# Reordering the first attention pair, and moving the rounding of the first output tile to GpSimd in the last one

## The chip, the cores and the metric

One core of a Trainium2 chip. The metric is the time of one execution of the program on the device, in microseconds (us); smaller is better. Everything here is about single microseconds out of 570.

## What is computed

A block of a transformer on 2 batches of 512 tokens with width 512, in float32. It is an attention with low-rank (latent) queries, keys and values, and then a gated feed-forward layer; before and after each of the two stands a layer norm, and the sum goes on.

```python
q = (rmsnorm(hidden @ Wq_a) * w) @ Wq_b             # 32 heads, 128 plain + 64 rotated columns
ckv = hidden @ Wkv_a                                # 64 latent + 64 rotated columns
q_pe, k_pe = rope(q_pe), rope(k_pe)
scores = (qf @ kf.T) * scale, causal
o = softmax(scores) @ v                             # 32 heads
return o @ Wo
...
x = x + layernorm(attention(layernorm(x)))
x = x + layernorm(ffn(layernorm(x)))                # silu(gate) * up, low-rank additions
```

## The kernel before

Each engine has its own program, written out by hand, with semaphores between them. There is no scheduler: an instruction that waits holds back all that stands behind it in its engine's program.

Float32 products are made of three products of rounded parts. A value is split into a rounded "hi" (a copy on ScalarE, or on VectorE) and a "lo" (the value less its hi, a subtraction on VectorE or GpSimd). `three` on TensorE then multiplies hi by hi, hi by lo and lo by hi.

The attention runs over 16 pairs of heads (`body(p)`). A pair has 16 steps k: eight for batch 0 and eight for batch 1, four query blocks for each of two heads. One unit of work is numbered U = 16p + k. Its stages, and the engines:

- `scores` (TensorE) makes the scores of unit U, two steps ahead of the step that turns them. Unit 4g (i = 0) needs the rotated query g (`pe_added`); unit 4g + 1 needs the query's lo part as well (`qt_split`). It also waits until the mask of unit U - 2 has emptied its bank (`s_masked`).
- `mask_and_max` (VectorE, L804) adds the causal mask and takes the row maximum. One input is in PSUM, the other in SBUF.
- `exponent` (ScalarE, L500), then `turn_p` (TensorE, L1249) transposes, `move_p` (ScalarE, L508) brings the result to SBUF, and `output` (TensorE, L1261) multiplies the values once for every eight units. `invert`, `turn_r`, `move_r` and `scale_o` divide by the row sums.

The queries of a pair come from `query` (TensorE, five products of 512 columns, L1179 to L1222). It needs the pair's weights in both parts: `weights_hi` (ScalarE, four roundings, L476 to L479), `weights_lo` (VectorE, L779 and L780), `rope_lo` (GpSimd, L395 and L398). A query is then rotated: `rotate_swapped` (VectorE, two half-tile products, L789 and L790), `rotate_own` (VectorE, L796), `add_rotated` (GpSimd, L382). Then it is split: `query_hi` (ScalarE, L490) and `query_lo` (GpSimd, L389). In the first pair, queries 0 and 1 (batch 0) are made in the stage before the attention; queries 2 and 3 (batch 1) are rotated and split inside `body(0)`, and queries 4 and 5 are the next pair's.

In the last pair (`last=True`) there is nothing left to prepare, so that work on the output projection is put in between: `split_weights` makes the parts of 16 projection weights (weights 0 to 5 wholly on VectorE, with a cast L826 and a subtraction L830; the rest with the rounding on ScalarE, L523), `split_output` splits a tile of the attention's output (L532 on ScalarE, L836 on VectorE, 1024 columns each), and `project` multiplies them on TensorE. The weights come back from a scratch in DRAM, through three buffers, in eight loads (L341): the load of weights 14 and 15 starts when weight 9 is split. `project(0, 0)` multiplies weights 0 to 7 with the first half of tile 0.

Of the kernel before, what the change touches and what calls it, by code (L numbers as in the profile page):

```python
# [20 lines left out]
F32 = mybir.dt.float32  # L21
# [65 lines left out]
def build(nc, x_d, wa_d, lnw_d, cst_d, kcs_d, sq_d, sv_d, w13_d, bs_d, a13_d, a2_d, w2_d, b2_d, out_d):  # L87
# [141 lines left out]
    def sems(phase, words):  # L229
        return Semaphores((n, nc.alloc_semaphore(f"{phase}_{n}")) for n in words.split())  # L230
# [12 lines left out]
    c = sems("projection", """xn2_made wv_in0 wv_in1 wv_in2 wv_copied wv_hi_made wv_split o_hi_made o_split o_used x1_first x1_in w13_in bs_in a13_in  # L243
# [9 lines left out]
    with block:  # L253
# [114 lines left out]
        def _(pool):  # L368
# [33 lines left out]
            def body(p, last=False):  # L402
                for b in (1,) if last else (1, 0):
                    for h in range(2):
                        gi = 4 * p + (2 if b else 4) + h
                        pool.wait_ge(a.qt_split, gi)
                        add_rotated(gi, h)
                        if b and h == 0 and not last:
                            pool.wait_ge(a.pe_added, gi + 1)
                            rope_lo(p + 1)  # L410
                        query_lo(gi, b, h, gi + 1)
# [22 lines left out]

# [27 lines left out]
        def _(act):  # L463
# [94 lines left out]
            def body(p, first=False, last=False):  # L558
                for k in range(PU):
                    if last and k == 6:  # L560
                        split_output(0, 0)
# [19 lines left out]
                    if k in ((2, 4) if first else (1, 4)):  # L581
                        h = k // 4
                        query_hi(4 * p + 2 + h, 1, h, None if first else PU * (p - 1) + UNITS + QB * (h + 1))
# [77 lines left out]
            exponent(1, 1, True)  # L661
            move_p(0, 0)
            exponent(2, 2, True)
            query_hi(1, 0, 1)
# [108 lines left out]
        def _(dve):  # L773
# [9 lines left out]
            def rotate_swapped(gi, h, first=False):  # L783

                dve.wait_ge(a.q_made, gi + 1)
                if not first:
                    dve.wait_ge(a.pe_added, gi - 1)
                G = bank[6 + h]
                nc.vector.tensor_tensor(qswp[64:96, h, :], G[96:128, :], sin1[96:128, :], ALU.mult)  # L789
                nc.vector.tensor_tensor(qswp[96:128, h, :], G[64:96, :], sin1[64:96, :], ALU.mult)  # L790
# [42 lines left out]
            def split_output(t, hh):  # L833

                dve.wait_ge(c.o_hi_made, 2 * t + hh + 1)
                nc.vector.tensor_tensor(o_s[:, hh, 1, :, :], ot[:, t, 8 * hh:8 * hh + 8, :],  # L836
                                        o_s[:, hh, 0, :, :].bitcast(F32), ALU.subtract).then_inc(c.o_split, 1)
# [8 lines left out]
            def body(p, first=False, last=False):  # L846
                for k in range(PU):
# [7 lines left out]
                    if last and k == 7:  # L855
                        split_output(0, 0)
# [3 lines left out]
                    if k < UNITS or not last:  # L860
                        if first and k in (1, 2):
                            rotate_swapped(gi + k - 1, k - 1)
                            if k == 1:
                                rotate_own(gi, 0)
                        elif first and k == 3:
                            weights_lo(p + 1)
                            rotate_own(gi + 1, 1)
# [34 lines left out]
            for t in range(TB + 4):  # L902
                if 2 <= t - 2 < TB:
                    turned_lo(t - 2)
                if 0 <= t - 3 < TB:
# [28 lines left out]
                if t == 7:  # L934
                    weights_lo(0)
                if 0 <= t - 4 < TB:
# [13 lines left out]
                if t in (TB, TB + 3):  # L950
                    h = (t - TB) // 3
                    rotate_swapped(h, h, first=True)
                    rotate_own(h, h, first=True)
# [222 lines left out]
        def _(pe):  # L1176
# [230 lines left out]
            body(PAIRS - 1, last=True)  # L1407
            output(2 * PAIRS - 1, 1, range(QB))
# [14 lines left out]
            project(0, 0, (6, 7))  # L1423
# [165 lines left out]
```

## Time and profile before

| | us |
|---|---|
| median of 3 runs (lowest, highest) | 570.12 (569.55, 570.97) |
| the profiled execution | 569.77 |
| its span, first to last instruction | 568.20 |
| TensorE busy | 555.2 (98%) |
| VectorE busy | 444.4 (78%) |
| ScalarE busy | 396.7 (70%) |
| GpSimd busy | 212.3 (37%) |

The first pair runs from about 41 us to 60 us, the last from about 382 us to 406 us, and the projection follows. A busy share is an average over all of these; what a change is worth can only be read in the stretch where it acts. TensorE's clock was granted at 0.997 of full over the span.

### The profile page before, as it was taken

To read this page: it belongs to the slowest core of one execution; us is meant where nothing else is said; L and a number is where in the kernel's file an instruction comes from. 1 tells how busy PE (TensorE), PEld (TensorE's weight loads), DVE (VectorE), ACT (ScalarE), POOL (GpSimd) and SP (SyncE) were. 2 spreads that over 40 slices of the span, in tenths; PEclk is the share of its full clock that TensorE was granted. 3 is DMA by queue.
4 is the path that set the end of the run, shared out by engine and by line. 5 is a ranking of instruction groups with operands and counts; after the bars stand their busy time and mean duration, and the time that the engine had idled before them with its cause. 6 is when DMAs were issued, how large, how long until landed. Compare 5 with 4: busy or idle time off the path is not lost. (4 is left out here: it accounts for less than half of the span.)

```text
span 568.2 us, 10892 instructions
## 1 busy us (share of the span) xinstructions
PE 555.2 (98%) x3280; PEld 423.4 (75%) x3280; DVE 444.4 (78%) x1198; ACT 396.7 (70%) x1173; POOL 212.3 (37%) x221
## 2 busy tenths in 40 slices
PE   8999999999999999999999999999999999999996
PEld 7777778777787787778877877876778888755565
DVE  5978777787777777877787788788878989885476
ACT  4767778787888787878888887888745554274353
POOL 3225454344443543444445435533011112135730
PEclk9999999999999999999999999999999999999998
DMA  8911232213312222111102101004591000001003
GB/s 325 407 64 66 81 101 82 79 53 99 112 53 80 78 106 80 53 50 59 53 21 71 52 20 45 22 21 149 190 347 58 2 14 1 1 1 55 1 35 115
DMA packets 22025, 46.93 MB, mean 83 GB/s; under 512 B 2896, under 2 KB 5712, under 8 KB 21712
## 3 DMA queue, kind: packets, MB, share of 16 engines
q1 hardware_dynamic: 21968, 46.23, 23.7%
q8 instruction: 28, 0.46, 0.3%
q14 instruction: 29, 0.24, 0.1%
HBM read 39.80 MB, written 6.42 MB: 81 GB/s over the span
## 5 line engine op out<-in xcount | busy, mean ns | idle before, releaser
L804 DVE CUSTOM_DVE_ANT_0 ss<-bank,cst 128x128 f32<-128x128 f32 (+3 forms) x256 | 125.1, 489 | 71.8 <-PE bank L1181 40.3
L508 ACT ACTIVATE pt<-bank 128x128 f32<-128x128 f32 (+3 forms) x256 | 110.2, 430 | 62.7 <-PE bank L1249 62.3
L500 ACT ACTIVATE pr<-ss,small 128x128 f32<-128x128 f32 (+3 forms) x256 | 143.0, 558 | 7.1 <-DVE small L804 5.6
L382 POOL TENSOR_TENSOR qrot<-qrot,qswp 64x512 f32<-64x512 f32 x64 | 82.2, 1284 | 115.9 <-DVE qrot L796 113.5
L1249 PE MATMUL bank<-ident,pr 128*128 128x128 f32 x640 | 113.6, 275 | 0.6 <-ACT pr L500 0.5
L1249 PEld LDWEIGHTS bank<-ident,pr 128*128 128x128 f32 x640 | 78.5, 141 | 22.2 <-issue 5.3
L389 POOL TENSOR_TENSOR qt_lo<-qrot,qt_hi 128x384 fp32r<-128x384 f32 x64 | 64.6, 1009 | 71.1 <-ACT qt_hi L490 70.0
L1179 PE MATMUL bank<-kt_hi,qt_hi 128*128 128x256 f32 (+2 forms) x192 | 80.9, 421 | 1.4 <-POOL qt_lo L389 0.7
L1261 PE MATMUL bank<-pt,kvn 128*64 128x256 f32 (+3 forms) x512 | 75.2, 434 | 0.7 <-ACT pt L508 0.7
L1261 PEld LDWEIGHTS bank<-pt,kvn 128*64 128x64 f32 x512 | 38.6, 137 | 40.6 <-issue 28.2
L1181 PE MATMUL bank<-kt_hi,qt_lo 128*128 128x256 f32 (+2 forms) x192 | 65.1, 339 | 0.0
L1180 PE MATMUL bank<-kt_lo,qt_hi 128*128 128x256 f32 (+2 forms) x192 | 64.7, 337 | 0.0
L1179 PE MATMUL bank<-wv,o_s 128*128 128x512 f32 x128 | 51.5, 402 | 0.0
L1181 PE MATMUL bank<-wv,o_s 128*128 128x512 f32 x128 | 50.5, 395 | 0.0
L1180 PE MATMUL bank<-wv,o_s 128*128 128x512 f32 x128 | 50.4, 394 | 0.0
L500 ACT ACTIVATION_READ_ACCUMULATOR pr<-ss,small 128x1 f32 x256 | 49.7, 194 | 0.0
L789 DVE TENSOR_TENSOR qswp<-bank,cst 32x512 f32<-32x512 f32 x64 | 44.5, 696 | 2.0
L790 DVE TENSOR_TENSOR qswp<-bank,cst 32x512 f32<-32x512 f32 x64 | 44.2, 691 | 0.9
L796 DVE TENSOR_TENSOR qrot<-bank,cst 128x512 f32<-128x512 f32 x64 | 43.9, 686 | 0.1
L438 POOL TENSOR_TENSOR half<-xn 128x256 f32<-128x256 f32 x7 | 8.1, 1157 | 89.9 <-ACT xn L550 79.9
L1179 PEld LDWEIGHTS bank<-kt_hi,qt_hi 128*128 128x128 f32 x192 | 36.4, 190 | 4.8 <-issue 1.6
L1181 PEld LDWEIGHTS bank<-kt_hi,qt_lo 128*128 128x128 f32 x192 | 36.1, 188 | 2.8
(189 smaller groups left out, 1113.8 us busy)
## 6 DMA issues: line engine op xcount, KB each, us to landing
rsb<-rinv_scratch SPq DMA_DIRECT2D x64, 128.0 KB, 2.9
sv<-sv SPq DMA_DIRECT2D x9, 576.0 KB, 4.5
sqa<-sq SPq DMA_DIRECT2D x16, 320.0 KB, 3.2
wv_raw<-wvo_scratch SPq DMA_DIRECT2D x8, 512.0 KB, 4.2
sve<-sv SPq DMA_DIRECT2D x7, 576.0 KB, 9.6
wvo_scratch<-vs SPq DMA_DIRECT2D x10, 256.0 KB, 2.2
xa<-x SPq DMA_DIRECT2D x8, 256.0 KB, 6.0
sqr<-sq SPq DMA_DIRECT2D x16, 128.0 KB, 2.2
```

What stands on the lines that cost most here:

```text
L382: nc.gpsimd.tensor_tensor(qrot[RKV:P, h, :], qrot[RKV:P, h, :], qswp[RKV:P, h, :], ALU.add)\
L389: nc.gpsimd.tensor_tensor(qt_lo[:, b, h, P:SEQ], qrot[:, h, P:SEQ], qt_hi[:, b, h, P:SEQ].bitcast(F32), ALU.subtract)\
L500: nc.scalar.activation(pr[:, k % 4, 0:n], ss[:, RING[k], 0:n], ACT.Exp, bias=negmax[:, k % 8:k % 8 + 1], scale=-1.0, accum_out=rsum[:, k:k ...
L508: nc.scalar.activation(pt[:, b, h, 0:i + 1, i * P:(i + 1) * P], bank[2 + k % 2][:, 0:(i + 1) * P].rearrange("p (j q) -> p j q", q=P), ACT. ...
L789: nc.vector.tensor_tensor(qswp[64:96, h, :], G[96:128, :], sin1[96:128, :], ALU.mult)
L790: nc.vector.tensor_tensor(qswp[96:128, h, :], G[64:96, :], sin1[64:96, :], ALU.mult)
L804: nc.vector.tensor_tensor_reduce(out=ss[:, RING[k], 0:n], in0=bank[k % 2][:, 0:n], in1=mask[:, SEQ - n:SEQ], scale=-SCALE, scalar=3.4e38, ...
L1179: nc.tensor.matmul(out, w_hi, x_hi, start=start, stop=False)
L1180: nc.tensor.matmul(out, w_hi, x_lo, start=False, stop=False)
L1181: return nc.tensor.matmul(out, w_lo, x_hi, start=False, stop=stop)
L1249: last = nc.tensor.transpose(bank[2 + k % 2][:, j * P:(j + 1) * P], pr[:, k % 4, j * P:(j + 1) * P], ident[:, :])
L1261: last = nc.tensor.matmul(bank[4][RKV * h:RKV * (h + 1), j * P:SEQ], kvn[:, QB * b + j, 0:RKV], pt[:, b, h, j, j * P:SEQ], start=(j == 0), ...
```

## The change

In the first pair and just ahead of it:

- VectorE rotates query 1 earlier: its two half-tile products go, one each, ahead of the latent scaling in the two last steps but one of the first stage, and `rotate_own` ahead of the last latent split. Before, all three stood behind mask 1.
- VectorE takes queries 2 and 3 in pieces between the masks: query 2's own product goes from step 1 to step 3, query 3's two halves from step 2 to steps 4 and 5, its own product from step 3 to step 5, and `weights_lo(1)` from step 3 to step 4.
- ScalarE does `query_hi` of query 1 ahead of `move_p(0)` and the third exponent; `query_hi` of queries 2 and 3 goes from steps 2 and 4 to steps 5 and 7, behind the exponents of units 7 and 9.
- GpSimd does `rope_lo(1)` ahead of `add_rotated` of query 2, not behind it.

In the last pair:

- The split of the first output tile's first half leaves ScalarE (step 6) and VectorE (step 7). GpSimd does it behind its last query: two copies of 512 columns and a subtraction of 1024 columns.
- TensorE's `project(0, 0)` for weight 6 goes from behind the last values product to ahead of it.

```diff
                     for h in range(2):
                         gi = 4 * p + (2 if b else 4) + h
                         pool.wait_ge(a.qt_split, gi)
+                        if b and h == p == 0:
+                            rope_lo(1)
                         add_rotated(gi, h)
-                        if b and h == 0 and not last:
+                        if b and h == 0 and p and not last:
                             pool.wait_ge(a.pe_added, gi + 1)
                             rope_lo(p + 1)
                         query_lo(gi, b, h, gi + 1)
...
+            pool.wait_ge(a.q_made, 4 * PAIRS)
+            pool.wait_ge(a.o_scaled, PAIRS + 2)
+            for n in (slice(0, 4), slice(4, 8)):
+                nc.gpsimd.tensor_copy(o_s[:, 0, 0, n, :], ot[:, 0, n, :]).then_inc(c.first_hi_made, 1)
+            pool.wait_ge(c.first_hi_made, 2)
+            nc.gpsimd.tensor_tensor(o_s[:, 0, 1, :, :], ot[:, 0, 0:8, :], o_s[:, 0, 0, :, :].bitcast(F32), ALU.subtract)\
+              .then_inc(c.o_split, 1)
...
                 for k in range(PU):
-                    if last and k == 6:
-                        split_output(0, 0)
...
-                    if k in ((2, 4) if first else (1, 4)):
-                        h = k // 4
+                    if k in ((5, 7) if first else (1, 4)):
+                        h = k // 7 if first else k // 4
                         query_hi(4 * p + 2 + h, 1, h, None if first else PU * (p - 1) + UNITS + QB * (h + 1))
...
             exponent(1, 1, True)
+            query_hi(1, 0, 1)
             move_p(0, 0)
             exponent(2, 2, True)
-            query_hi(1, 0, 1)
...
-                dve.wait_ge(c.o_hi_made, 2 * t + hh + 1)
+                dve.wait_ge(c.o_hi_made, 2 * t + hh)
...
-                    if last and k == 7:
-                        split_output(0, 0)
...
-                        if first and k in (1, 2):
-                            rotate_swapped(gi + k - 1, k - 1)
+                        if first and 0 < k < 6:
                             if k == 1:
+                                rotate_swapped(gi, 0)
+                            if k == 3:
                                 rotate_own(gi, 0)
-                        elif first and k == 3:
-                            weights_lo(p + 1)
-                            rotate_own(gi + 1, 1)
+                            if k == 4:
+                                weights_lo(p + 1)
+                            if k in (4, 5):
+                                rotate_swapped(gi + 1, 1, parts=(k - 4,))
+                            if k == 5:
+                                rotate_own(gi + 1, 1)
...
+                if t in (TB + 1, TB + 2):
+                    rotate_swapped(1, 1, True, (t - TB - 1,))
...
+                if t == TB + 3:
+                    rotate_own(1, 1, first=True)
...
-                if t in (TB, TB + 3):
-                    h = (t - TB) // 3
-                    rotate_swapped(h, h, first=True)
-                    rotate_own(h, h, first=True)
+                if t == TB:
+                    rotate_swapped(0, 0, first=True)
+                    rotate_own(0, 0, first=True)
...
             body(PAIRS - 1, last=True)
+            project(0, 0, (6,))
             output(2 * PAIRS - 1, 1, range(QB))
...
-            project(0, 0, (6, 7))
+            project(0, 0, (7,))
```

## Rows read from the trace of the kernel before

**Rows 1.** Busy time by stretch: start:end, length, then PE, PEld, DVE, ACT, POOL

```profile
60.00:383.00 323.00, 323.00 (x2101) 252.96 (x2098) 250.61 (x714) 260.55 (x852) 143.69 (x143) 1.00 0.20 64
```

**Rows 2.** Waits of TensorE, 41 to 60 us: total, times, longest

```profile
PE bank L1179 <- POOL qt_lo L389: 0.7, 1, 0.7
PE bank L1179 <- DVE small L804: 0.6, 1, 0.6
```

**Rows 3.** Timeline of TensorE, first pair and second: start, duration, instruction, idle before

```profile
46.23 0.49 PE L1249 MATMUL bank<-ident,pr 128*128 128x128 f32 x3
...
50.60 0.39 PE L1179 MATMUL bank<-ql_hi,w_hi 128*128 128x512 f32 x1
...
51.75 0.38 PE L1249 MATMUL bank<-ident,pr 128*128 128x128 f32 x2
...
52.55 0.36 PE L1179 MATMUL bank<-kt_hi,qt_hi 128*128 128x256 f32 x1
...
56.59 0.46 PE L1235 MATMUL bank<-kt,qrot 128*128 128x128 f32 x2
...
76.45 0.37 PE L1179 MATMUL bank<-kt_hi,qt_hi 128*128 128x256 f32 x1
...
80.13 0.39 PE L1235 MATMUL bank<-kt,qrot 128*128 128x128 f32 x2
```

**Rows 4.** Timeline of VectorE, end of the first stage and first pair

```profile
36.12 0.17 DVE L912 RECIPROCAL st<-st 128x2 f32<-128x2 f32 x1 [0.86 <-ACT st L624]
...
47.58 0.28 DVE L804 CUSTOM_DVE_ANT_0 ss<-bank,cst 128x128 f32<-128x128 f32 x1
```

**Rows 5.** Timeline of ScalarE, first pair

```profile
48.30 0.29 ACT L476 ACTIVATE w_hi<-sqr 128x128 fp32r<-128x128 f32 x1
...
52.70 0.52 ACT L490 ACTIVATE qt_hi<-qrot 128x384 fp32r<-128x384 f32 x1 [0.50 <-POOL qrot L382]
...
53.39 0.71 ACT L500 ACTIVATE pr<-ss,small 128x512 f32<-128x512 f32 x1
```

**Rows 6.** Timeline of GpSimd, first pair

```profile
53.36 1.02 POOL L389 TENSOR_TENSOR qt_lo<-qrot,qt_hi 128x384 fp32r<-128x384 f32 x1 [0.70 <-ACT qt_hi L490]
```

**Rows 7.** Waits of TensorE, 383 to 415 us

```profile
PE bank L1261 <- ACT pt L508: 0.7, 1, 0.7
PE bank L1270 <- ACT pr L500: 0.5, 1, 0.5
```

**Rows 8.** Timeline of VectorE, last pair and after it

```profile
392.01 1.23 DVE L836 TENSOR_TENSOR o_s<-ot,o_s 128x1024 fp32r<-128x1024 f32 x1 [0.74 <-ACT o_s L532]
...
393.63 0.42 DVE L826 CAST wv<-wv_raw 128x512 fp32r<-128x512 f32 x1
...
401.88 0.69 DVE L830 TENSOR_TENSOR wv<-wv_raw,wv 128x512 fp32r<-128x512 f32 x1
...
413.42 1.23 DVE L836 TENSOR_TENSOR o_s<-ot,o_s 128x1024 fp32r<-128x1024 f32 x1 [0.18 <-ACT o_s L532]
```

**Rows 9.** GpSimd's instructions by line and shape: total busy us, mean ns of one

```profile
L389 POOL TENSOR_TENSOR qt_lo<-qrot,qt_hi 128x384 fp32r<-128x384 f32 x64 | 64.6, 1009 | 71.1 <-ACT qt_hi L490 70.0
...
L395 POOL TENSOR_TENSOR w_lo<-sqr,w_hi 128x128 fp32r<-128x128 f32 x16 | 7.4, 460 | 8.9 <-ACT w L477 8.9
...
L419 POOL COPY qn<-qn 128x64 f32<-128x64 f32 x8 | 1.9, 238 | 0.0
```

**Rows 10.** Timeline of GpSimd, then of VectorE, 420 to 426 us

```profile
422.50 1.14 POOL L438 TENSOR_TENSOR half<-xn 128x256 f32<-128x256 f32 x1 [31.30 <-ACT xn L550]
...
422.97 1.23 DVE L1000 CUSTOM_DVE_ANT_0 dot<-xn,a 128x512 f32<-128x512 f32 x1
```

**Rows 11.** Timeline of TensorE, end of the last pair and projection

```profile
403.13 0.48 PE L1179 MATMUL bank<-wv,o_s 128*128 128x512 f32 x1
...
414.70 0.50 PE L1179 MATMUL bank<-wv,o_s 128*128 128x512 f32 x1
```

**Rows 12.** Timeline of ScalarE, start of the projection

```profile
411.28 1.16 ACT L523 ACTIVATE wv<-wv_raw 128x512 fp32r<-128x512 f32 x2 [1.11 <-DMA wv_raw<-wvo_scratch]
```

More of the change, by code:

```diff
@@ L242, in build @@
         wvo_made wvo_moved wvo_out""")
-    c = sems("projection", """xn2_made wv_in0 wv_in1 wv_in2 wv_copied wv_hi_made wv_split o_hi_made o_split o_used x1_first x1_in w13_in bs_in a13_in
+    c = sems("projection", """xn2_made wv_in0 wv_in1 wv_in2 wv_copied wv_hi_made wv_split first_hi_made o_hi_made o_split o_used x1_first x1_in w13_in bs_in a13_in
         dve_step std1_made z_made std2_made half_made fold_made dots_raw dots_made lt_zero y_turned xt2_moved lp_hi_made lp_split""")
@@ L781, in weights_lo, with rotate_swapped @@
                   .then_inc(a.wq_split, 1)
-            def rotate_swapped(gi, h, first=False):
+            def rotate_swapped(gi, h, first=False, parts=(0, 1)):
                 dve.wait_ge(a.q_made, gi + 1)
@@ L787, in rotate_swapped @@
                     dve.wait_ge(a.pe_added, gi - 1)
-                G = bank[6 + h]
-                nc.vector.tensor_tensor(qswp[64:96, h, :], G[96:128, :], sin1[96:128, :], ALU.mult)
-                nc.vector.tensor_tensor(qswp[96:128, h, :], G[64:96, :], sin1[64:96, :], ALU.mult)
+                for j in parts:
+                    to, of = 64 + 32 * j, 96 - 32 * j
+                    nc.vector.tensor_tensor(qswp[to:to + 32, h, :], bank[6 + h][of:of + 32, :], sin1[of:of + 32, :], ALU.mult)
             def rotate_own(gi, h, first=False):
```

## The prediction, made before the changed kernel was run

> **What bounds the kernel now.** I read the busy times by stretch first. From 60 to 383 us TensorE is busy for 323.00 of 323.00 us [rows 1]: there it is the bound, it has no gap, and whatever delay it has at 60 us it still has at 383. So I then read TensorE's waits in the two stretches that the change touches. In the first pair they are 0.7 us for the lo part of query 1 and 0.6 us for a mask [rows 2]; at the end of the last pair 0.5 us before the transposed row sums and 0.7 us for the last `move_p` [rows 7]. That is all there is to win: some 2.5 us, plus a little refill of the pipeline. Then I walked through both stretches by the timelines of the engines, since every one of these waits ends a chain over VectorE, ScalarE and GpSimd, and the change reorders those chains.
>
> **Query 1, earlier.** Its rotation costs VectorE three products. They go into gaps: one half into 0.86 us in which VectorE waits for ScalarE [rows 4], the others into two like it of 0.72 and 1.06 us in the next two steps; a half takes 0.70 us, so they just fit, and cost nothing. If a gap were missed, what is late is a latent split, by some 0.1 us. The own product is then ready by 40.8 us, GpSimd adds by 42.1, and the lo part is done at about 44.4 instead of 47.4. The score product of unit 5 can start 0.25 us behind the transposes at 46.23 [rows 3] instead of at 47.46: TensorE is 1.0 us ahead.
>
> **Up to query 4.** Mask 4 no longer has query 2's own product (0.61 us) in front of it and starts at 47.0 instead of 47.58 [rows 4]. Exponent 4 and `weights_hi(1)` behind it on ScalarE are 0.6 us earlier too: 47.7 instead of 48.30 [rows 5], done 0.8 us later at 48.5. VectorE is free for `weights_lo(1)` (two of 0.3 us) at 48.7 and done at 49.3. On GpSimd `rope_lo(1)`, two of 0.46 us [rows 9], starts 0.15 us behind the rope roundings at 48.2 and is done at about 49.35, since it now goes ahead of the addition. So query 4 starts at 49.4 instead of 50.60 [rows 3]. TensorE waits there for 0.7 us, and is 1.2 us ahead. `add_rotated` of query 2, now behind `rope_lo`, is done at 50.7, just when the score product of unit 8 wants it (50.8): no loss.
>
> **Unit 9, the place where it turns.** That product needs the lo part of query 2. Before, its rounding stood at step 2 of ScalarE's program, long ahead. Now it stands at step 5, behind `move_p(5)` and the exponent of unit 7, and `move_p(5)` needs transposes that TensorE makes behind query 4. The chain from query 4's start: 1.15 us to the transposes (50.60 to 51.75) [rows 3] and 0.38 until they are done, 51.0; on ScalarE the move, the exponent (0.71) and the rounding (0.52), 0.69 of which are the step from 52.70 to 53.39 [rows 5], so 1.5 us in all, 52.5; 0.15 us and 1.02 us on GpSimd [rows 6], 53.7. Before, the product started at 52.55 [rows 3]. Without this chain it could start at 51.3; with it TensorE stands for 2.4 us and comes out 1.15 us behind the kernel before. From 52.55 to 56.59 the kernel before takes 4.04 us for pieces that take 3.68 us in the second pair (76.45 to 80.13) [rows 3]; these 0.36 us are small waits that a later TensorE doesn't meet. So the first pair costs 0.8 us, with 1.2 us as the upper end (nothing given back) and 0.4 us as the lower (each of the five hand-overs of the chain 0.08 us shorter). The rounding of query 3, behind exponent 9, has slack: its lo part is ready at 58.6, and unit 13 comes at 61.
>
> **The first output tile on GpSimd.** ScalarE loses its 1.05 us, so that exponent 8 starts almost 1 us earlier and the 0.5 us wait at the row sums [rows 7] is gone: TensorE is 0.8 us ahead from 392.1 us. VectorE loses 1.23 us at 392.01 [rows 8], but mask 10 behind it needs scores that are ready at 392.3, so it gains 0.9. GpSimd starts at 391.3, behind its last `query_lo`. The subtraction: 384 columns take 1.009 us and 128 take 0.460 [rows 9], 2.15 ns a column, so 1024 take 2.4 us. A copy of 512 columns isn't in the trace. Lower bound 0.6 us (0.238 for 64 columns [rows 9], the other 448 at 0.8 ns); upper bound 1.3 us (the subtraction's rate). I take 0.75, as the one copy that is there takes three quarters of a short two-input instruction but has one input to read. The copies end at 392.8, the subtraction at 395.3 to 395.7. Weight 0's product wants it at 396.6: in time, up to copies of 1.2 us. *A page's price:* the Trainium skill, GPSIMD Engine Reference, § 3.1, gives 769 ns for 512 elements of a tight one-input loop; by that the sum is the same 571.6.
>
> **What GpSimd's subtraction does to VectorE.** In the projection GpSimd's addition starts at 422.50 and lasts until 423.64; VectorE's instruction with both inputs in SBUF starts at 422.97 and takes 1.23 us instead of its 0.69, that is it ends 0.55 us behind GpSimd's end [rows 10]. So VectorE stood until GpSimd was through. Masks and rotations have one input in PSUM and keep their durations beside GpSimd all through the attention. In the last pair VectorE starts splitting weights behind mask 10: cast and subtraction, both from SBUF. With the cast at 392.8 and GpSimd's subtraction starting at about 392.9 either way round, weight 0's parts are done at about 396.2 and mask 11 starts there, instead of at 394.69: VectorE is 1.5 us late. And it has no slack: from 393.15 to 404.4 it goes from mask to split to mask with gaps of 0.2 us in all. Weight 5's lo part was done at 402.57, 0.56 us ahead of its product at 403.13 [rows 8, 11]. So 1.5 less 0.2 less 0.56: TensorE is 0.7 us late at weight 5's product, and its 0.8 us lead is lost on the way. Bounds: 0.8 us early (VectorE isn't held up), 1.7 us late (copies of 1.3 us, cast and subtraction both held up). 
>
> **Weight 6's product ahead of the last values.** 0.7 us of TensorE's work goes into its 0.7 us wait for `move_p(15)` [rows 7]. But the gain isn't kept: the first product of tile 1, at 414.70 [rows 11], starts right behind the split of that tile, which ends at 413.42 + 1.23 = 414.65 [rows 8]. This split hangs on ScalarE's last two weights, which wait 1.11 us for their load [rows 12], which waits for weight 9's split, which is behind `move_p(15)`. That chain starts at the transposes of unit 15 and doesn't become shorter. TensorE comes to it 0.7 us early and waits: 0 us gained, 0.1 at most.
>
> **Sum.** +0.8 + 0.7 + 0 = +1.5 us. The profiled execution took 569.77 us, 568.20 of them its span; it becomes 571.3. The median of the runs is 0.35 us above it, so I forecast 571.6 us, and by the ends of the terms (0.4 less 0.8, and 1.2 and 1.7) 569.7 to 573.0, its own likely range 570.8 to 572.4. A measurement of this kernel tells a change of about 0.3%, 1.7 us, from none.
>
> **Rivals.**
>
> 1. *GpSimd doesn't hold up VectorE.* For: most of GpSimd's work in the attention costs VectorE nothing. Against: the instruction at 422.97 [rows 10]. The last pair then keeps its 0.8 us lead, the first costs 0.8: 570.1 us. Chance 0.2.
> 2. *It does what it says.* The lo part of query 2 comes in time and so all four waits go: 1.0 + 0.6 + 0.8 + 0.7 us, 567.0 us. It needs the rounding of query 2 to be done 2.4 us earlier than its place in ScalarE's program allows. Chance 0.1.
> 3. *Slower: VectorE becomes the bound of the last pair.* With copies of 1.2 us or more, GpSimd holds the port to 396.6; VectorE is 2.5 us late, and TensorE waits at the scores of unit 13 and again at weights 4 and 5: +1.7 us there, +1.0 in the first pair, 572.8 us. It decides from the point where cast and subtraction both wait, copies of about 1.0 us. Chance 0.2.
>
> The forecast has 0.45; 0.05 is left for what I don't see. Faster by over 0.3% (below 568.4) holds rival 2: 0.1. Slower by over 0.3% (above 571.8) holds rival 3 and four tenths of the forecast: 0.38. The rest, 0.52, is no change. For 8 in 10 the range runs from 569.0, which takes in rival 1, to 573.0.
>
> **What would show it.** First pair: TensorE's wait for `qt_lo` moves from unit 5 to unit 9 and grows to 2.4 us; query 4 starts 1.2 us earlier; the product of unit 12 starts 0.8 us later than 56.59. Last pair: GpSimd's subtraction takes 2.4 us or more; one cast or subtraction of VectorE near 393 us takes over 2 us; mask 11 starts at 396.2; no wait for ScalarE's row sums; TensorE waits for VectorE's weight 5, and for the split of tile 1. The prediction is wrong in sign if unit 9 doesn't wait, or if VectorE's weight splits keep 0.42 and 0.69 us.

## The result, and the profile after

The changed kernel takes 572.71 us (median of 5 runs, 571.00 to 573.21); the kernel before took 569.97 us in the runs beside it. The ratio is 1.0041, 95% interval 1.003 to 1.0051: slower by 0.4%. The forecast was 571.6 us, in a range of 569.0 to 573.0. One execution each of three kernels further below (the second form of both mended halves, weight 6 alone, the subtraction in halves) took 689 to 1931 us, and the ratios leave these three out.

| | before | after |
|---|---|---|
| span of the profiled execution, us | 568.2 | 570.7 |
| TensorE busy, us | 555.2 | 557.7 |
| VectorE, ScalarE, GpSimd busy, us | 444.4, 396.7, 212.3 | 444.9, 395.4, 215.8 |

TensorE is busy for 2.5 us longer although it executes the same 3280 matmuls. 0.8 us of that lies in the first 10 us, ahead of every edit (8.47 against 7.67 us busy), but 1.3 us lies between the first latent transposes and unit 12 (21.27 against 19.97). That is the first sign that it isn't only a matter of waits: a wait makes an engine idle, not busy. All line numbers have moved in the changed kernel: the helper `three`, L1179 to L1181 before, is L1191 to L1193, `turn_p` (L1249) is L1261, and the unit products L1235 are L1247.

**First pair.** TensorE's waits from 41 to 62 us, in total, times, longest (before: [rows 2]):

```profile
PE bank L1191 <- POOL qt_lo L389: 2.2, 1, 2.2
PE bank L1191 <- DVE w L787: 0.5, 1, 0.5
```

The wait for a lo part is no longer at unit 5, but at unit 9, three times as long. TensorE's timeline shows what it does around it (start, duration, instruction, idle before and its releaser; before: [rows 3]):

```profile
46.73 0.49 PE L1261 MATMUL bank<-ident,pr 128*128 128x128 f32 x3
46.98 0.36 PE L1191 MATMUL bank<-kt_hi,qt_hi 128*128 128x256 f32 x1
...
49.97 0.47 PE L1191 MATMUL bank<-ql_hi,w_hi 128*128 128x512 f32 x1 [0.54 <-DVE w L787]
...
54.30 0.39 PE L1191 MATMUL bank<-kt_hi,qt_hi 128*128 128x256 f32 x1 [2.17 <-POOL qt_lo L389]
...
55.54 0.63 PE L1193 MATMUL bank<-ql_hi,w_lo 128*128 128x512 f32 x1
55.97 0.63 PE L1233 MATMUL bank<-ql_hi,w 128*128 128x512 f32 x1
...
59.59 0.39 PE L1247 MATMUL bank<-kt,qrot 128*128 128x128 f32 x2
```

Unit 5 now follows its transposes by 0.25 us. Query 4 is 0.63 us earlier than before, unit 9 is 1.75 us later. And then come two lines that a list of waits doesn't have: products of 512 columns that take 0.63 us and follow each other by 0.43 us, where the same ones at 50.50 us took 0.39 and followed by 0.23. From unit 9 to unit 12 TensorE needs 59.59 − 54.30 = 5.29 us for pieces that take 3.68 us in the second pair [rows 3]. The windows of this stretch say why (start:end, length, then busy time of PE, PEld, DVE, ACT, POOL, the granted clock of TensorE, and DMA):

```profile
50.00:52.00 2.00, 2.00 (x12) 1.63 (x12) 1.94 (x5) 1.16 (x6) 1.24 (x1) 1.00 0.45 101
52.00:54.00 2.00, 0.13 (x2) 0.00 (x0) 0.81 (x3) 1.87 (x6) 0.75 (x1) 1.00 0.33 128
54.00:56.00 2.00, 1.71 (x7) 1.42 (x8) 1.02 (x4) 0.00 (x0) 1.52 (x2) 0.70 0.00 0
56.00:58.00 2.00, 2.00 (x9) 1.70 (x7) 0.91 (x2) 0.09 (x1) 0.00 (x0) 0.50 0.00 0
58.00:60.00 2.00, 2.00 (x14) 1.62 (x15) 1.34 (x4) 2.00 (x7) 0.44 (x1) 0.94 0.00 0
```

and of the kernel before, in the two that matter:

```profile
54.00:56.00 2.00, 2.00 (x14) 1.53 (x12) 1.72 (x4) 2.00 (x9) 0.38 (x1) 1.00 0.00 0
56.00:58.00 2.00, 1.98 (x12) 1.00 (x12) 1.97 (x6) 1.62 (x7) 0.81 (x1) 1.00 0.01 2
```

The granted clock is 0.70 and 0.50 behind the standstill. 0.50 is half of full speed, 1.2 GHz in place of 2.4; 0.70 is the mean of a window that began at full speed. Before it fell, TensorE had stood still from 52.13 to 54.30. The Trainium skill (TensorE: Matmul & The Clock Gate, Part 1) names the same two levels, and an idle stretch as what leads to the lower one; the trace agrees as to both, 0.50 behind a wait of 2.17 us.

The chain that makes unit 9 wait, on ScalarE and then on GpSimd (before: [rows 5, 6]):

```profile
51.62 0.38 ACT L517 ACTIVATE pt<-bank 128x256 f32<-128x256 f32 x1 [0.84 <-PE bank L1261]
51.90 0.71 ACT L509 ACTIVATE pr<-ss,small 128x512 f32<-128x512 f32 x1
...
52.60 0.51 ACT L499 ACTIVATE qt_hi<-qrot 128x384 fp32r<-128x384 f32 x1
```

```profile
53.25 0.99 POOL L389 TENSOR_TENSOR qt_lo<-qrot,qt_hi 128x384 fp32r<-128x384 f32 x1 [2.01 <-ACT qt_hi L499]
```

ScalarE stands before `move_p(5)` for transposes that TensorE makes behind query 4, and the rounding of query 2 is queued behind it.

**Last pair.** GpSimd's new copies and its subtraction, then VectorE (before: [rows 8, 9]):

```profile
394.01 1.17 POOL L440 CAST o_s<-ot 128x512 fp32r<-128x512 f32 x2
395.26 2.38 POOL L442 TENSOR_TENSOR o_s<-ot,o_s 128x1024 fp32r<-128x1024 f32 x1
```

```profile
395.65 2.27 DVE L833 CAST wv<-wv_raw 128x512 fp32r<-128x512 f32 x1
...
398.57 0.68 DVE L811 CUSTOM_DVE_ANT_0 ss<-bank,cst 128x512 f32<-128x512 f32 x1
399.18 0.08 DVE L811 DVE_READ_ACCUMULATOR2_ANT small<- 128x1 f32 x1
399.18 0.42 DVE L833 CAST wv<-wv_raw 128x512 fp32r<-128x512 f32 x1
```

One and the same cast takes 0.42 us at 399.18 and 2.27 us at 395.65, where it ends 0.28 us behind GpSimd's subtraction (395.26 + 2.38 = 397.64, 395.65 + 2.27 = 397.92). Mask 11 stands behind it.

Weight 5's product and tile 1's first product on TensorE, and the load behind tile 1 on ScalarE (before: [rows 11, 12]):

```profile
406.37 0.48 PE L1191 MATMUL bank<-wv,o_s 128*128 128x512 f32 x1 [0.47 <-DVE wv L837]
...
417.38 0.39 PE L1191 MATMUL bank<-wv,o_s 128*128 128x512 f32 x1
```

```profile
413.84 1.16 ACT L532 ACTIVATE wv<-wv_raw 128x512 fp32r<-128x512 f32 x2 [0.33 <-DMA wv_raw<-wvo_scratch]
```

**Where the time went.** The same instruction of TensorE stands in both traces, so the difference of its two starts is the delay up to there, and the steps between are the cost of each stretch. The first row, the start-up, is by how much the whole trace is later ahead of any edit:

| up to | before | after | delay | step | forecast |
|---|---|---|---|---|---|
| first latent transposes | 35.04 | 35.26 | 0.22 | start-up | – |
| transposes ahead of unit 5 | 46.23 | 46.73 | 0.50 | +0.28 | 0 |
| query 4 | 50.60 | 49.97 | −0.63 | −1.13 | −1.2 |
| unit 9 | 52.55 | 54.30 | 1.75 | +2.38 | +2.35 |
| unit 12 | 56.59 | 59.59 | 3.00 | +1.25 | −0.36 |
| turn of the last pair | 386.41 | 389.28 | 2.87 | −0.13 | 0 |
| weight 5's product | 403.13 | 406.37 | 3.24 | +0.37 | +0.7 |
| tile 1's first product | 414.70 | 417.38 | 2.68 | −0.56 | 0 |

### The profile page after: what moved, and what is told of

It reads as the page before. It is cut to its first block, busy times and chain, and to the rows that moved or that the text cites. A ratio compares the mean times of both kernels' runs of the same rounds, so it can differ in the third digit from the quotient of the medians.

```text
span 570.7 us, 10896 instructions
## 1 busy us (share of the span) xinstructions
PE 557.7 (98%) x3280; PEld 425.4 (75%) x3280; DVE 444.9 (78%) x1197; ACT 395.4 (69%) x1172; POOL 215.8 (38%) x224
## 3 DMA queue, kind: packets, MB, share of 16 engines
q1 hardware_dynamic: 21968, 46.23, 23.7%
## 4 chain that ended last, share of the span: by engine, by line
PE 81%; DVE 12%; ACT 3%; issue 3%; POOL 0%; DVEq 0%; POOLq 0%; ACTq 0%
PE bank L1191 14%; PE bank L1193 13%; PE bank L1192 13%; PE bank L1261 12%; PE bank L1273 12%; DVE dot L1012 3%; PE bank L1288 3%; PE bank L1234 3%; PE bank L1233 3%; PE bank L1247 2%; PE bank L1213 1%; DVE st L986 1%; DVE o_s L843 1%; PE bank L1471 1%; ACT o_s L541 1%
## 5 line engine op out<-in xcount | busy, mean ns | idle before, releaser
L1261 PE MATMUL bank<-ident,pr 128*128 128x128 f32 x640 | 113.9, 276 | 0.6 <-ACT pr L509 0.5
L1261 PEld LDWEIGHTS bank<-ident,pr 128*128 128x128 f32 x640 | 79.0, 141 | 22.0 <-issue 5.5
L1191 PE MATMUL bank<-kt_hi,qt_hi 128*128 128x256 f32 (+2 forms) x192 | 81.2, 423 | 2.3 <-POOL qt_lo L389 2.2
L1193 PE MATMUL bank<-kt_hi,qt_lo 128*128 128x256 f32 (+2 forms) x192 | 65.0, 339 | 0.0
L1191 PE MATMUL bank<-wv,o_s 128*128 128x512 f32 x128 | 51.6, 403 | 0.5 <-DVE wv L837 0.5
L1193 PE MATMUL bank<-wv,o_s 128*128 128x512 f32 x128 | 50.5, 395 | 0.0
L1191 PEld LDWEIGHTS bank<-kt_hi,qt_hi 128*128 128x128 f32 x192 | 36.6, 190 | 5.7 <-POOL qt_lo L389 2.4
L1193 PEld LDWEIGHTS bank<-kt_hi,qt_lo 128*128 128x128 f32 x192 | 36.2, 188 | 2.8
L1192 PEld LDWEIGHTS bank<-kt_lo,qt_hi 128*128 128x128 f32 x192 | 37.0, 193 | 0.0
```

The source lines that it names most:

```text
L1191: nc.tensor.matmul(out, w_hi, x_hi, start=start, stop=False)
L1192: nc.tensor.matmul(out, w_hi, x_lo, start=False, stop=False)
L1193: return nc.tensor.matmul(out, w_lo, x_hi, start=False, stop=stop)
L1261: last = nc.tensor.transpose(bank[2 + k % 2][:, j * P:(j + 1) * P], pr[:, k % 4, j * P:(j + 1) * P], ident[:, :])
```

## The experiments

Two theories stood at the start. A: the whole loss is made in the first pair, by the wait at unit 9 and by the lower clock behind it, and the last pair costs next to nothing. B: the last pair, through VectorE's held-up cast, costs its share of some 0.7 us. Each kernel was timed in rounds with the kernel before on the same chip (its median was 570.0 or 570.1 us in each of the three series).

### The first pair alone, the last pair alone

The change has two halves that touch different stretches; each kernel here is the kernel before with one of them (the hunks on `rotate_swapped`, `rotate_own`, `query_hi`, `rope_lo` and `weights_lo` in the one, the rest in the other).

> The kernel before with the edits of the first pair alone. Theory A (what the trace of the changed kernel says): the pieces moved ahead cost 0.25 us, the chain to the score product of unit 9 costs 0.8 us, and TensorE's clock at half speed behind the long wait costs 1.6 us, so +2.6 us: about 572.6 us, with the product of unit 12 about 2.7 us later than in the kernel before. Theory B (the slow stretch of the clock is not tied to the wait, an accident of that execution): only the chain, +1.0 us, 571.0 us.

> The kernel before with the edits of the last pair alone. Theory A: weight 6's product does fill the wait, and the load of the last weights comes 0.6 us sooner behind its trigger than I reckoned, so that the pair ends 0.2 us early: 569.8 us, TensorE's first product of tile 1 at 414.5. The forecast's reckoning: +0.7 us, 570.7 us, that product at 415.4, with TensorE waiting for the split of tile 1.

Measured: 572.88 us for the first pair alone, ratio 1.005 (1.0033 to 1.0066), and 570.36 us for the last pair alone, ratio 1.0006 (0.9997 to 1.0016). The first pair alone makes the whole loss, near the 572.6 us of theory A. Its windows show the lower clock again, and its timeline shows it from the first product behind the wait (0.29 us to the next product where the changed kernel has 0.22):

```profile
54.00:56.00 2.00, 1.67 (x6) 1.47 (x7) 0.68 (x4) 0.00 (x0) 1.55 (x2) 0.61 0.00 0
56.00:58.00 2.00, 2.00 (x9) 1.60 (x8) 1.26 (x2) 0.00 (x0) 0.00 (x0) 0.53 0.00 0
```

```profile
54.33 0.49 PE L1188 MATMUL bank<-kt_hi,qt_hi 128*128 128x256 f32 x1 [2.17 <-POOL qt_lo L389]
54.62 0.42 PE L1189 MATMUL bank<-kt_lo,qt_hi 128*128 128x256 f32 x1
```

In the last pair alone the cast is held up in the same way, and TensorE comes to tile 1's first product 0.53 us behind the kernel before, having entered the pair 0.30 us behind it: the pair costs 0.23 us net. I had expected this pair either to end 0.2 us early or to cost 0.7 us. It does neither: the product is at 415.23, behind a wait of 0.28 us for its split, and the interval of the time holds no change.

```profile
393.08 2.25 DVE L831 CAST wv<-wv_raw 128x512 fp32r<-128x512 f32 x1
...
395.98 0.68 DVE L809 CUSTOM_DVE_ANT_0 ss<-bank,cst 128x512 f32<-128x512 f32 x1
```

### Is it the standstill that costs, or what comes of it?

The wait and the clock come together. To part them, TensorE gets work without a use in the wait; the wait itself isn't touched. This is the changed kernel with

```diff
                     n = k + 2
+                    if first and n == 9:
+                        for _ in range(20):
+                            nc.tensor.transpose(bank[XB][:, 0:P], ident[:, :], ident[:, :])
                     if n < PU:
```

> The changed kernel, and on TensorE 20 transposes of the identity (0.11 us each, 2.1 us in all) ahead of the score product of unit 9, so that TensorE works while it waits. Nothing else changes, and the product still starts when its lo part is there. Theory A (the clock falls because TensorE stands still): the granted clock stays at 1.0 from 54 to 59 us, the pieces behind unit 9 take 3.7 us and not 5.3, and the time is 1.6 us below the changed kernel's: 571.1 us. Theory B (something else slows these pieces): the clock falls again and the time is the changed kernel's, 572.7 us.

Measured: 571.64 us, ratio 1.0021 (1.0004 to 1.0039), 1.1 us less than the changed kernel though TensorE does more. The two intervals overlap (1.003 to 1.0051 for the changed kernel), so it is the trace that decides. The timeline of TensorE:

```profile
51.95 2.35 PE L1322 MATMUL bank<-ident 128*128 128x128 f32 x20
54.30 0.39 PE L1191 MATMUL bank<-kt_hi,qt_hi 128*128 128x256 f32 x1
...
55.22 0.39 PE L1193 MATMUL bank<-ql_hi,w_lo 128*128 128x512 f32 x1
...
58.00 0.28 PE L1247 MATMUL bank<-kt,qrot 128*128 128x128 f32 x1
```

Unit 9 starts at 54.30, as in the changed kernel, but unit 12 is at 58.00 and no longer at 59.59; the pieces take 3.70 us, the 3.68 us of the second pair, and a product of 512 columns takes 0.39 us. The granted clock is 1.00 in all windows from 52 to 60 us. The standstill itself costs 2.2 us, and the clock that it leads to costs 1.6 us on top. That is shown for these traces: nothing but the idleness was taken away. I had expected 571.1 us. TensorE is still 1.56 us ahead of the changed kernel at the turn of the last pair (387.72 against 389.28), but only 1.21 us at tile 1's first product (416.17 against 417.38), where it waits 0.21 us for its split, behind a load of the last weights that took 0.5 us longer (below).

The lower clock may not come in every execution. Of the five timed ones of the changed kernel, four took 572.35 to 573.21 us at a mean granted clock of 0.994 to 0.997, and the fifth took 571.00 us at 0.999. That is what a run without the fall would give, but no trace of it was kept.

### Rounding one step earlier

The wait is a matter of one place in ScalarE's program. The changed kernel with

```diff
-                    if k in ((5, 7) if first else (1, 4)):
+                    if k in ((4, 7) if first else (1, 4)):
```

> The changed kernel with the rounding of query 2 on ScalarE at step 4 in place of 5, that is ahead of the move of unit 5 and the exponent of unit 7. Theory A (the place of the rounding makes the wait): the addition is done at 51.25, the rounding at 51.8, the lo part at 53.0, so that TensorE waits 0.9 us at unit 9 and not 2.2; 1.3 us less, and if the clock stays up another 1.6: 570.0 us, or 571.4 if it falls even so. Theory B (GpSimd's order, the rope part ahead of the addition, makes the wait): the lo part comes at 54 as before, 572.7 us.

Measured: 569.94 us, ratio 1.0001 (0.9991 to 1.001). One digit takes the whole loss back, as theory A had it. The rounding now stands ahead of `move_p(5)` and its wait for TensorE; unit 9 still waits, but its wait of 0.85 us doesn't bring the clock down (1.00 in all windows from 52 to 58 us):

```profile
52.94 0.38 PE L1191 MATMUL bank<-kt_hi,qt_hi 128*128 128x256 f32 x1 [0.85 <-POOL qt_lo L389]
...
56.67 0.39 PE L1247 MATMUL bank<-kt,qrot 128*128 128x128 f32 x2
```

Unit 12 is at 56.67 against 56.59 before.

### Query 1 alone

What is the early rotation of query 1 worth? The kernel before with the hunks for query 1 only (its two halves and its own product in the first stage, its rounding ahead of `move_p(0)`).

> The kernel before with one edit alone: the rotation of query 1 is done early, in pieces, and its rounding stands ahead of move_p(0); the order inside the first pair stays. Theory B (the lo part of query 1 isn't the last thing late): the 0.7 us wait at unit 5 is gone, but query 4 still waits for its weights, whose chain over mask 4, exponent 4 and the roundings is unchanged, so it starts within 0.3 us of 50.60 on the trace; the three pieces ahead of the first latent scaling cost the 0.25 us that the changed kernel shows there, or nothing if TensorE waits for the weights in any case. Time 570.0 to 570.3. Rival: unit 5's gain is kept, query 4 starts at 49.6 to 49.9 and the time is 569.0 to 569.4.

Measured: 570.25 us, ratio 1.0003 (0.9994 to 1.0012). TensorE's waits and timeline:

```profile
PE bank L1182 <- DVE small L804: 1.4, 2, 1.0
```

```profile
46.87 0.36 PE L1182 MATMUL bank<-kt_hi,qt_hi 128*128 128x256 f32 x1
...
50.99 0.40 PE L1182 MATMUL bank<-ql_hi,w_hi 128*128 128x512 f32 x1
```

Unit 5 follows its transposes by 0.25 us in place of 1.23, so 1.0 us is gained there, and by query 4 it is all given back, 50.99 against 50.60 (0.29 us later, net of a start-up of 0.10), in waits for VectorE's masks: the wait for `qt_lo` has turned into waits for `small`. At the turn of the last pair this kernel is 0.2 us later than the start-up accounts for, which is the price of the three early pieces. So an early query 1 gains nothing by itself. That it pays together with what makes query 4 earlier is likely, but not shown: no run has the rest without it.

### The first pair with the chain in another order

If the two chains (weights to query 4, query 2 to unit 9) set the pair, both must be shortened. Both kernels are the kernel before with the change's first-pair hunks, and these steps in place of its own (`weights_hi(1)`, then `query_hi`, then VectorE's pieces inside the pair, and query 1's in the first stage):

```diff
-                    if k == (2 if first else 1) and not last:
+                    if k == 1 and not last:
...
-                    if k in ((2, 4) if first else (1, 4)):
+                    if k in ((3, 7) if first else (1, 4)):
...
+                            if k == 2:
+                                rotate_own(gi, 0)
+                            if k == 3:
+                                weights_lo(p + 1)
...
+                if t == TB + 1:
+                    rotate_swapped(1, 1, True, (0,))
...
+                if t == TB + 3:
+                    rotate_swapped(1, 1, True, (1,))
+                    rotate_own(1, 1, first=True)
```

This is the second of them; the first has query 2's own product at step 3 and its rounding at step 4.

> The edits of the first pair alone, with other steps: query 2's and 3's rounding at steps 4 and 7, weights_hi(1) on ScalarE at step 1 and weights_lo(1) on VectorE at step 3, and query 1's second half behind the latent scaling rather than ahead of it. Theory (first pair is a chain over weights, query 4, and the rounding of query 2; the clock falls only if TensorE stands for long at unit 9): query 4 starts at 48.9 to 49.5, unit 9 at 51.6 to 52.3 with a wait under 1.2 us, granted clock 1.00, so 0.3 to 0.9 us ahead of the kernel before: 569.1 to 569.7. Rival (each us gained in front is given back by the rounding): unit 9 at 52.9 as with step 4 alone, 569.9 to 570.1.

> As the run before, with query 2's own product at step 2 and its rounding at step 3. Theory: unit 9 at 50.9 to 51.5, 1.0 to 1.5 us ahead of the kernel before, 568.6 to 569.1. Rival: the own product in front of mask 3 makes the scores of unit 5 or the turn of unit 4 late, weights and query 4 follow, and the gain is under 0.5 us: 569.5 to 570.0.

Measured: 569.34 us, ratio 0.9986 (0.9978 to 0.9995), and 569.33 us, ratio 0.9986 (0.9977 to 0.9994). TensorE in the second:

```profile
49.41 0.40 PE L1189 MATMUL bank<-ql_hi,w_hi 128*128 128x512 f32 x1
...
51.43 0.39 PE L1189 MATMUL bank<-kt_hi,qt_hi 128*128 128x256 f32 x1
...
52.68 0.47 PE L1189 MATMUL bank<-ql_hi,w_hi 128*128 128x512 f32 x1 [0.63 <-DVE qrot L798]
```

Query 4 is 1.2 us and unit 9 1.1 us earlier than before, and unit 9 doesn't wait. What is late next is query 5: its product overwrites the bank from which VectorE still reads query 3, whose pieces now stand at steps 4 and 5. Both kernels are 1.0 us ahead of the start-up's offset at the turn of the last pair, 0.7 us in the time. My expectations for the places in the first were missed (query 4 at 48.9 to 49.5, unit 9 at 51.6 to 52.3): they are at 49.96 and 52.82, but its whole trace is 1.1 us late from the start-up on. Its time was met. For the second it is the other way round: unit 9 at 51.43 was met, and the time of 569.33 us lies between the 568.6 to 569.1 of the theory and the 569.5 to 570.0 of its rival. One step earlier for query 2 didn't show in the time, since query 5 is the next to wait.

### GpSimd's copies in its own gap

The last pair's edits alone, but with GpSimd's two copies ahead of its last `query_lo`, in the 1.5 us for which it stands there:

```diff
+                        if last and h:
+                            pool.wait_ge(a.q_made, 4 * PAIRS)
+                            pool.wait_ge(a.o_scaled, PAIRS + 2)
+                            pool.wait_ge(a.pe_added, gi + 1)
+                            for n in (slice(0, 4), slice(4, 8)):
+                                nc.gpsimd.tensor_copy(o_s[:, 0, 0, n, :], ot[:, 0, n, :]).then_inc(c.first_hi_made, 1)
+                            pool.wait_ge(c.first_hi_made, 2)
                         query_lo(gi, b, h, gi + 1)
```

> The kernel before with the edits of the last pair alone, but with GpSimd's two copies ahead of its last query_lo, in the 1.5 us in which it stands for the rounding, so that its subtraction starts some 1.2 us earlier (about 391.5). Theory (the time of the last pair's edit hangs on how long GpSimd's subtraction holds VectorE's first cast): the cast takes 0.9 to 1.4 us instead of 2.25, mask 11 is at 394.6 to 395.0, TensorE doesn't wait for weight 5, and its entry offset of 0 to 0.3 us is what is left: 569.3 to 569.9. Rival (the load of the last weights sets the end of this stretch whatever the masks do): the cast is shorter but tile 1's first product stays at 414.7 to 415.2, 570.0 to 570.4.

Measured: 569.25 us, ratio 0.9992 (0.9978 to 1.0005). GpSimd, VectorE and TensorE:

```profile
389.10 1.17 POOL L416 CAST o_s<-ot 128x512 fp32r<-128x512 f32 x2 [0.16 <-POOL qrot L382]
...
391.58 2.39 POOL L443 TENSOR_TENSOR o_s<-ot,o_s 128x1024 fp32r<-128x1024 f32 x1
```

```profile
393.06 1.20 DVE L834 CAST wv<-wv_raw 128x512 fp32r<-128x512 f32 x1
...
394.90 0.68 DVE L812 CUSTOM_DVE_ANT_0 ss<-bank,cst 128x512 f32<-128x512 f32 x1
```

```profile
414.11 0.50 PE L1185 MATMUL bank<-wv,o_s 128*128 128x512 f32 x1 [0.24 <-DVE o_s L844]
```

The subtraction starts 1.10 us earlier (391.58 against 392.68) and the cast, at the same place to 0.02 us, becomes 1.05 us shorter. In each of the three traces (and in the two of both mended halves) the cast ends 0.28 or 0.29 us behind GpSimd's subtraction. So the hold-up is a matter of where the subtraction ends, not of how much GpSimd does. Tile 1's first product is 0.59 us ahead of the kernel before and was 0.27 us behind on entry, so the last pair gains 0.9 us. Places and theory agree; the time is just under the 569.3 to 569.9 us that I had expected, and its interval alone doesn't part this kernel from the one before.

### Weight 6's product alone

The kernel before with `project(0, 0, (6,))` ahead of the last `output`, `(7,)` behind it, and nothing else.

> The kernel before with one edit alone: weight 6's product ahead of the last values. Theory of the prediction (the split of tile 1 behind the load of the last weights sets the end): the wait for move_p(15) is gone, weight 8's product is 0.6 to 0.7 us earlier, tile 1's first product waits for its split and stays within 0.15 us of 414.70 plus the entry offset; time 570.0 to 570.2. Rival (the load comes earlier too, as the runs of the last pair alone hint): tile 1's product at 414.1 to 414.4, 569.4 to 569.7.

Measured: 569.87 us, ratio 0.9996 (0.9986 to 1.0006). TensorE, and ScalarE's last weights:

```profile
408.59 0.50 PE L1179 MATMUL bank<-wv,o_s 128*128 128x512 f32 x1
...
414.83 0.50 PE L1179 MATMUL bank<-wv,o_s 128*128 128x512 f32 x1 [0.35 <-DVE o_s L836]
```

```profile
411.42 1.16 ACT L523 ACTIVATE wv<-wv_raw 128x512 fp32r<-128x512 f32 x2 [1.10 <-DMA wv_raw<-wvo_scratch]
```

Weight 8's product is 0.4 us earlier (409.00 before; 0.5 us net of the delay on entry, where I had expected 0.6 to 0.7), tile 1's first product is where it was (414.83 against 414.70, with 0.12 us of entry delay), behind a new wait for the split. Taken alone the edit is worth nothing, as forecast.

### The subtraction in halves

The last pair's edits as in the change, with the subtraction in two instructions of 512 columns.

> The edits of the last pair as in the change, but GpSimd's subtraction of 1024 columns made in two instructions of 512. Theory (VectorE's cast is held for what is left of the one GpSimd instruction that runs, not for a queue of them): GpSimd's first half takes 1.2 us, and the cast that meets it takes 0.9 to 1.4 us instead of 2.25; GpSimd's second half and VectorE's subtraction then take turns, so mask 11 is at 395.0 to 396.3 instead of 396.1 and the time 569.6 to 570.3. Rival (GpSimd keeps VectorE out over both halves): the cast takes 2.2 us or more again and the time is 570.2 to 570.6.

Measured: 570.23 us, ratio 0.9996 (0.9986 to 1.0005), against 570.36 us (1.0006, 0.9997 to 1.0016) in one piece. The intervals overlap, the time is within the span that both theories gave, and there is no trace from which the places could be read, so whether the cast is held over both halves stays open.

### Both mended halves together

> Both edits in their mended form in one kernel: the first pair as in the run with query 2's own product at step 2, the last pair as in the run with GpSimd's copies ahead of its last lo part. Theory (TensorE has no gap from 60 to 383 us, so what the two ends gain adds up): minus 0.7 and minus 0.8 us, 568.5 to 568.8. Rival (an earlier TensorE at the last pair meets an end that is set by the load of the last weights, so the second gain is smaller): 569.0 to 569.4.

> The same with the other form of the first pair (own product at step 3, rounding at step 4). Both theories as for the run before; 568.5 to 568.8 if the gains add up, 569.0 to 569.4 if the load of the last weights takes one back.

Measured: 568.07 us, ratio 0.996 (0.9944 to 0.9975), and 568.38 us, ratio 0.9964 (0.995 to 0.9978). Both beat the kernel before and the changed one. The gains add up: in the first, TensorE enters the last pair 1.25 us ahead of the kernel before (385.16 against 386.41; 1.04 us net of the start-up) and comes to tile 1 2.53 us ahead:

```profile
412.17 0.41 PE L1195 MATMUL bank<-wv,o_s 128*128 128x512 f32 x1
```

```profile
408.67 1.16 ACT L535 ACTIVATE wv<-wv_raw 128x512 fp32r<-128x512 f32 x2 [0.34 <-DMA wv_raw<-wvo_scratch]
```

The times are 0.4 and 0.1 us below the lower end of what I expected. The load of the last weights waited for is shorter here (below), which helps in the trace; the interval of the time, −1.4 to −3.2 us, holds the sum of the two parts (−1.5 us) as well.

## Why the prediction was right, and where its sum was not

The sign and the range held, and so did the place: the wait for `qt_lo` moves to unit 9. Most terms of the first pair came out to a tenth of a microsecond. But two terms were wrong in opposite directions, and the sum of 1.5 us was too small against 2.7 us in the medians (2.3 us by the ratio). That the time stayed inside the range is in part luck: the first pair cost more than twice its own upper end of 1.2 us, and the range had room for it only because it held 1.7 us for a last pair that cost next to nothing.

- **Query 1, early: cost put at 0, 0.1 at most.** It costs 0.2 to 0.3 us: the transposes ahead of unit 5 are 0.28 us later than the start-up accounts for, and in the run with query 1 alone 0.2 us stay. The pieces fitted into VectorE's idle time, but the latent scaling behind them came a little late, and TensorE shows a new 0.27 us wait for `qn` at 37.85 us.
- **Up to query 4: −1.2 us, measured −1.13.** Right, with `weights_lo` done at 49.73 and `rope_lo` as the last to come at 49.87 (I had 49.35, and the trace was 0.50 us late there), a wait of 0.54 us. The profile puts the wait down to `weights_lo`, but by their ends it is `rope_lo`.
- **Unit 9: wait of 2.4 us, 1.15 us behind.** Measured 2.17 us and, net of the 0.50 us on entry, 1.25 us behind. The chain was priced hand-over by hand-over, and held: move at 51.62, rounding at 52.60, lo part at 53.25. The experiment that moves the rounding by one step confirms the mechanism: the loss is gone.
- **From unit 9 to unit 12: 0.36 us given back.** This is the step that failed. It took TensorE's pieces at the durations of the second pair and so took the clock for granted. The row shows 1.25 us lost in place of 0.36 gained; with TensorE kept busy through the same wait the pieces take 3.70 us, so the forecast of their own length was right, and all of the 1.6 us is the clock (1.25 and the missing 0.36). The first pair thus costs 2.65 us (3.00 less the start-up's 0.22 and the 0.13 given back by 386 us) where I had 0.8. A clock of 0.997 over the span, which I had noted, says nothing of a stretch that is made idle only by the change.
- **No split of tile 0 on ScalarE: 0.8 us ahead.** Right. The wait of 0.5 us at the row sums is gone, and TensorE's delay falls from 2.87 us at the turn to 2.07 us at the next one (398.73 against 396.66); the lead is then lost at weight 5, as forecast.
- **GpSimd holds up VectorE: +1.5 us at mask 11, +0.7 at weight 5's product.** The mechanism was right: cast 2.27 us, subtraction 2.38 us. The Trainium skill's rule (SBUF — State Buffer, Who interferes with whom), that the shared ports are locked for a whole instruction, agrees with the cast of 1.20 us that ends with GpSimd's in the run with the copies in the gap; rival 1, no hold-up, is refuted. The size was off: the two copies took 1.17 us together and not 1.5, and started 0.2 us earlier than I had it (394.01 less 2.87, against 391.3), so mask 11 was 1.0 us late (398.57 against 394.69, less 2.87 of entry) and weight 5's product 0.37 us. The 769 ns that the Trainium skill (GPSIMD Engine Reference, § 3.1) gives for 512 elements is above what this copy took, 0.58 us.
- **Weight 6's product: 0.** Right by its own run: the split of tile 1 binds, tile 1's product doesn't move. In the changed kernel it was wrong: the product fills the wait for `move_p(15)`, weight 8's product is 0.56 us closer to its old place (411.68 against 409.00, 2.68 late in place of 3.24), and this gain is kept, since TensorE doesn't wait for tile 1's split there. The chain to the load is as late as weight 5's product (VectorE's weights 8 and 9 at 408.93 against 405.70, +3.23), but from there to ScalarE's first use of the load it is 3.6 us (408.93 + 1.29 to 413.84), where it was 4.3 us before (406.99 to 411.28). I had taken the load's duration as fixed.
- **Rival 3** (VectorE the bound of the last pair) needed copies of 1.0 us or more; they took 0.6. The time of 572.7 us is near the 572.8 that it gave, but for another reason; its last pair did not happen. **Rival 2** needed the rounding earlier than its place allows. Moved to an earlier place, it comes in time.

What stays open is why the clock stays at half for as long as it does, whether it falls in every execution, and the load's spread.

## What to carry to other kernels

Price a new wait of the engine that is the bound twice: once for its length, once for what follows if the clock falls behind it; a wait of 0.85 us here cost its length, one of 2.17 us cost 1.6 us more. When a step is put later in an in-order program, look at what stands directly ahead of it and whether that waits for the very engine that will wait for the step: here one step earlier was worth 2.8 us. And work handed to an idle engine should go where that engine stands idle, and end as early as it can before the neighbour that it holds up starts: 1.1 us earlier took 1.05 us off VectorE's cast.

## What the runs showed of the hardware that I had not expected

- TensorE's granted clock fell to 0.50 (1.2 of 2.4 GHz) behind a standstill of 2.17 us. In the changed kernel it fell when TensorE was already busy again (the first products behind the wait have their usual distance, they are 0.37 us apart at 54.75 and 0.42 to 0.43 from 55.12 on), with the first pair alone from the first product on; the usual distance is back at about 58.3 and 57.9 us. The two traces with this wait show it; those that wait 0.63 to 0.97 us around the same place, and the one with the wait filled, don't.
- The same load of 512 KB, issued by the same instruction, reached ScalarE 3.6 to 3.8 us behind the end of VectorE's split of weight 9 in four traces (the changed kernel, the rounding at step 4 and both combined ones) and 4.1 to 4.4 us behind it in the nine others. The four have the edits of both halves, but so has the one with the filled wait, at 4.1 us. I know no cause.
- A copy of 512 columns with rounding takes 0.58 us on GpSimd (I had put it at 0.75), and a subtraction of 1024 columns, with its two inputs, 2.38 us: four times as long for twice the columns.
